# An S4 and SwiGLU layer on one core: other order and other first factors at the start of the kernel

## The reference, cut to what matters

```python
x  = u.reshape(2048, 512)                       # 2 x 1024 rows
xn = (x - mean(x)) / sqrt(var(x) + 1e-5)        # over 512 columns
# S4: a convolution along the 512 columns, kernel K from 64 complex states
B  = Vc @ Bp                                    # 64x64 complex by 64 real
K  = ifft(2/(1+Om) * (k00 - k01 * k10 / (1 + k11))).real   # Cauchy sums over Lambda, p, q, Ct, B
s  = causal_conv(xn, K) + D * xn
# FFN, hidden 1376, LoRA rank 16, scaling 2
lin(x, w, a, b) = x @ w.T + 2 * (x @ a.T) @ b.T
h  = silu(lin(xn, w1, A1, B1)) * lin(xn, w3, A3, B3)
out = x + s * silu(lin(h, w2, A2, B2))
```

## Time and profile before

| what | value |
|---|---|
| median of three runs | 411.93 us |
| the profiled execution, its own time | 412.15 us |
| its span, first to last instruction | 410.4 us |
| PE busy, records | 405.3 us (99%), 1860 |
| DVE busy | 164.9 us (40%) |
| ACT busy | 107.1 us (26%) |
| POOL busy | 66.8 us (16%) |
| DMA, whole span | 26.2 MB, mean 64 GB/s |
| granted TensorE clock by slice | 9 in all forty slices (9 is 90% or more) |

### The profile page before, as it was taken

How to read it: one execution, slowest core, us unless ns; L and a number is a source line. 1 busy time by engine, 2 the same in 40 slices (tenths; PEclk the granted TensorE clock), 3 DMA queues, 4 the chain that set the end, 5 groups by cost and what they waited for, 6 DMA issues and landing times.

```text
span 410.4 us, 5012 instructions
## 1 busy us (share of the span) xinstructions
PE 405.3 (99%) x1860; PEld 338.6 (83%) x1860; DVE 164.9 (40%) x259; ACT 107.1 (26%) x176; POOL 66.8 (16%) x130
## 2 busy tenths in 40 slices
PE   8999999999999999999999999999999999999996
PEld 8988888888888888888888888888888888888885
DVE  5777775654693321232244222132334212211125
ACT  7554333322441111122221111212222111111122
POOL 6227627330700114000000101400000000000000
PEclk9999999999999999999999999999999999999999
DMA  8663943220516101000006101000002000000002
GB/s 274 161 218 101 306 133 80 82 90 20 153 52 206 51 2 52 2 0 0 0 29 215 66 0 52 0 0 0 0 0 102 2 0 0 2 0 0 2 0 102
DMA packets 14338, 26.20 MB, mean 64 GB/s; under 512 B 2560, under 2 KB 4608, under 8 KB 14320
## 3 DMA queue, kind: packets, MB, share of 16 engines
q1 hardware_dynamic: 13872, 24.85, 18.9%
q0 software_dynamic: 160, 0.59, 0.4%
q10 hardware_dynamic: 288, 0.52, 0.3%
HBM read 20.33 MB, written 4.53 MB: 61 GB/s over the span
## 4 chain that ended last, share of the span: by engine, by line
PE 91%; DVE 4%; DMA 2%; issue 1%; ACT 1%; SPq 0%; POOL 0%; DVEq 0%; POOLq 0%
PE h L936 19%; PE h L935 19%; PE h L934 19%; PE f L935 10%; PE f L934 10%; PE f L936 10%; PE h L957 2%; DMA trig_sb<-trig_dram 2%; PE h L965 1%; PE spare L921 1%; DVE raw L732 1%; DVE w L747 1%; PE spare L936 1%; PE spare L935 1%; PE spare L934 1%
## 5 line engine op out<-in xcount | busy, mean ns | idle before, releaser
L934 PE MATMUL h<-xt,w 128*128 (+2 forms) x340 | 131.5, 387 | 0.0
L935 PE MATMUL h<-xt,w 128*128 (+2 forms) x340 | 131.1, 386 | 0.0
L936 PE MATMUL h<-xt,w 128*128 (+2 forms) x340 | 131.1, 386 | 0.0
L936 PEld LDWEIGHTS h<-xt,w 128*128 128x128 f32 x340 | 63.9, 188 | 12.8
L935 PEld LDWEIGHTS h<-xt,w 128*128 128x128 f32 x340 | 63.9, 188 | 12.7
L934 PEld LDWEIGHTS h<-xt,w 128*128 128x128 f32 x340 | 63.9, 188 | 12.6
L796 DVE TENSOR_TENSOR g<-g,h 128x512 f32<-128x512 f32 x40 | 27.5, 688 | 111.1 <-PE h L936 110.9
L801 DVE TENSOR_TENSOR ghl<-g,ghl 128x512 fp32r<-128x512 f32 x44 | 31.6, 719 | 92.5 <-ACT ghl L625 92.5
L934 PE MATMUL f<-ghl,w2f 128*128 128x512 f32 x176 | 68.6, 390 | 0.0
L625 ACT CAST ghl<-g 128x512 fp32r<-128x512 f32 x44 | 27.3, 621 | 157.9 <-PE f L936 144.7
L935 PE MATMUL f<-ghl,w2f 128*128 128x512 f32 x176 | 68.6, 389 | 0.0
(11 more groups left out here) (131 smaller groups left out, 306.2 us busy)
## 6 DMA issues: line engine op xcount, KB each, us to landing
raw<-w_dram SPq DMA_DIRECT2D x28, 256.0 KB, 3.4
xres<-xT_dram SPq DMA_DIRECT2D x4, 1024.0 KB, 7.2
outT_dram<-xres SPq DMA_DIRECT2D x15, 256.0 KB, 2.4
rows_next<-x_dram SPq DMA_DIRECT2D x4, 512.0 KB, 3.6
scale_rows<-scales_scratch SPq DMA_DIRECT2D x3, 512.0 KB, 4.1
rows<-x_dram SPq DMA_DIRECT2D x2, 512.0 KB, 6.8
raw<-w_dram SPq DMA_DIRECT2D x4, 224.0 KB, 2.4
lora_stack<-lora_spread_split SPq DMA_DIRECT2D x3, 204.0 KB, 3.7
```

The costliest lines, as they stand in the source:

```text
L934: pe.matmul(out, w[1], m[0], start=start, stop=False)
L935: pe.matmul(out, w[0], m[1], start=False, stop=False)
L936: return pe.matmul(out, w[0], m[0], start=False, stop=stop)
```

## The change

Seven edits, which all concern block 0:

1. Tile 0 of w2 joins `FOLD_FIRST`: it is folded with plain factors. `lr` grows from 1536 to 2176 columns, and its clearing with it; DVE clears 1216 columns for 832.
2. `folds`: (2,0) leaves the gate of j = 1, and (3,3) moves from the up of j = 2 to the down of j = 1.
3. SP: the raw tile (1,0) is loaded ahead of the first factors, not behind them; trig and the raw tile (2,1) are loaded ahead of the six stacking DMAs.
4. ACT and DVE: the order of their work up to the first hidden tile.
5. TensorE: the order of `start()`, with `fold(2,0)` in it.
6. Bp and Vc: two products over 64 partitions for one over 128.
7. `TOEPLITZ_AT` from (9, "up") to (8, "up"), and POOL's second `rows_rstd(1, 2)` behind the split of tz.

```diff
-FIRST_COLS = {1: 2 * D, 3: 2 * D + 2 * P}
-LORA_FIRST = 2 * D + 4 * P
+FIRST_COLS = {1: 2 * D, 3: 2 * D + 2 * P, 2: 2 * D + 5 * P}
+LORA_FIRST = 3 * D + 5 * P
-FACTORS_BY_DVE = 832
-PLAIN = {1: 1, 3: 1, 2: -1}
+FACTORS_BY_DVE = 1216
+PLAIN = {1: 1, 3: 1, 2: 0}
-FOLD_FIRST = [(1, 0), (3, 0), (1, 1), (3, 1)]
+FOLD_FIRST = [(1, 0), (3, 0), (1, 1), (3, 1), (2, 0)]
     if j == 1:
-        return {"gate": [(2, 0), (1, 2)], "up": [(3, 2), (1, 3)], "down": [(2, 1)]}[place]
-    if j == 2:
-        return {"gate": [(1, 4)], "up": [(3, 3), (3, 4)], "down": [(2, 2)]}[place]
+        return {"gate": [(1, 2)], "up": [(3, 2), (1, 3)], "down": [(2, 1), (3, 3)]}[place]
-TOEPLITZ_AT = (9, "up")
+TOEPLITZ_AT = (8, "up")
...
@@ sync
             load_tile(0)
+            load_raw(1, 0)
             sync.wait_ge(factors_dve, 1)
             sync.wait_ge(factors_pool, 1)
             sync.dma_start(lr[0:P:STACK_STEP, :], lora).then_inc(lora_in, 16)
             sync.dma_start(lane_c[:, :], lanes).then_inc(const_in, 16)
-            load_raw(1, 0)
...
             sync.dma_start(vc_sb[:, :], s4_vc).then_inc(bvec_in, 16)
+            sync.dma_start(trig_sb[:, :, :].rearrange("p a l -> p (a l)"), trig.to_broadcast([P, 2 * D])) \
+                .then_inc(s4_in, 16)
+            load_raw(2, 1)
...
-            early = [(1, 2), (3, 2), (1, 3), (2, 1), (3, 3)]
-            for kind, j in early[:2]:
-                load_raw(kind, j)
-            sync.dma_start(trig_sb[:, :, :].rearrange("p a l -> p (a l)"), trig.to_broadcast([P, 2 * D])) \
-                .then_inc(trig_in, 16)
-            for kind, j in early[2:]:
+            early = [(1, 2), (3, 2), (1, 3), (3, 3)]
+            for kind, j in early:
                 load_raw(kind, j)
@@ scalar
+            rows_hi(0)
             fold_hi(1, 0)
-            rows_hi(0)
+            rows_hi(1)
+            fold_hi(3, 0)
             act.wait_ge(spread_in, 32)
             nc.scalar.copy(spread_hl[:, 0, :], spread[:, :]).then_inc(spread_hi, 1)
             rows_norm(2)
-            rows_hi(1)
             rows_norm(3)
-            fold_hi(3, 0)
             rows_hi(2)
+            fold_hi(1, 1)
             rows_hi(3)
-            fold_hi(1, 1)
             fold_hi(3, 1)
+            fold_hi(2, 0)
             hidden(0, 0)
@@ vector
             fold_add(3, 0)
+            rows_lo(0)
             fold_lo(1, 0)
-            rows_lo(0)
+            rows_lo(1)
             dve.wait_ge(spread_hi, 1)
             nc.vector.tensor_tensor(spread_hl[:, 1, :], spread[:, :], spread_hl[:, 0, :].bitcast(F32), ALU.subtract) \
                 .then_inc(spread_lo, 1)
-            rows_lo(1)
             fold_lo(3, 0)
+            fold_add(1, 1)
+            fold_add(3, 1)
             rows_lo(2)
             rows_lo(3)
-            fold_add(1, 1)
-            fold_add(3, 1)
             fold_lo(1, 1)
             fold_lo(3, 1)
+            fold_add(2, 0)
+            fold_lo(2, 0)
             hidden_mul(0, 0)
@@ tensor, start()
                 fold(1, 0)
-                fold(3, 0)
                 pe.wait_ge(const_in, 16)
                 turn_rows(0)
+                fold(3, 0)
+                turn_rows(1)
                 fold(1, 1)
-                turn_rows(1)
-                fold(3, 1)
-                turn_rows(2)
 
                 pe.wait_ge(whi_done, 1)
                 pe.wait_ge(xhi_done, RT // 2)
...
-                turn_rows(3)
+                fold(3, 1)
                 wait_split(pe, 1, 0)
                 pe.wait_ge(xlo_done, RT // 2)
...
+                turn_rows(2)
+                turn_rows(3)
                 wait_split(pe, 3, 0)
                 hidden(0, 0, 0, 3, h3, lo)
+                fold(2, 0)
                 pe.wait_ge(xlo_done, RT)
                 hidden(0, 0, 0, 1, h1, hi).then_inc(h1_ready, 1)
...
-                pe.matmul(bankt[:, 0:2], vc_sb[:, :], bp_sb[:, :], start=True, stop=True).then_inc(b_ready, 1)
+                for ri in range(2):
+                    mm = pe.matmul(bankt[:, ri:ri + 1], vc_sb[:, ri * P:(ri + 1) * P], bp_sb[:, :], start=True, stop=True)
+                mm.then_inc(b_ready, 1)
@@ gpsimd
             rows_rstd(1, 0)
-            rows_rstd(1, 2)
             pool.wait_ge(tz_hi, 1)
             tt(tzs[:, 1, :], tz[:, :], tzs[:, 0, :].bitcast(F32), ALU.subtract).then_inc(tz_lo, 1)
-            pool.wait_ge(tz_lo, 1)
+            rows_rstd(1, 2)
```

More of the change, by code:

```diff
@@ L140 @@
 STACK_STEP = P // R
-FACTORS_BY_DVE = 832
-PLAIN = {1: 1, 3: 1, 2: -1}
-A_FIRST = {1: 0, 3: D}
-FOLD_FIRST = [(1, 0), (3, 0), (1, 1), (3, 1)]
+FACTORS_BY_DVE = 1216
+PLAIN = {1: 1, 3: 1, 2: 0}
+A_FIRST = {1: 0, 3: D, 2: 2 * D + 4 * P}
+FOLD_FIRST = [(1, 0), (3, 0), (1, 1), (3, 1), (2, 0)]
 def folds(place, j):
@@ L279, in build @@
         scales = put("scales", [P, 2, RT])
-        bp_sb = put("bp_sb", [P, 2])
+        bp_sb = put("bp_sb", [NS, 1])
         scal = put("scal", [P, 2])
@@ L308, in build @@
         even_odd = put("even_odd", [P, 2, D // 2])
-        vc_sb = put("vc_sb", [P, P])
+        vc_sb = put("vc_sb", [NS, 2 * P])
         krow = put("krow", [P, P + D])
@@ L347, in build @@
         spread_in, stack_in, stack_cleared = sem("spread_in"), sem("stack_in"), sem("stack_cleared")
-        s4_in, trig_in, bvec_in, dft_in = sem("s4_in"), sem("trig_in"), sem("bvec_in"), sem("dft_in")
+        s4_in, bvec_in, dft_in = sem("s4_in"), sem("bvec_in"), sem("dft_in")
         res0_in, res_in = sem("res0_in"), sem("res_in")
@@ L525, in _ @@
             sync.dma_start(spread[:, LANES_ST:LANES_ST + LANES_MV], lora_mv).then_inc(spread_in, 16)
-            for kind, j in FOLD_FIRST[2:] + [(2, 0)]:
+            for kind, j in FOLD_FIRST[2:]:
                 load_raw(kind, j)
@@ L539, in _ @@
                                    spread_hl[:, hl, lane_cols].bitcast(F32)).then_inc(stack_in, 16)
-            early = [(1, 2), (3, 2), (1, 3), (2, 1), (3, 3)]
-            for kind, j in early[:2]:
-                load_raw(kind, j)
-            sync.dma_start(trig_sb[:, :, :].rearrange("p a l -> p (a l)"), trig.to_broadcast([P, 2 * D])) \
-                .then_inc(trig_in, 16)
-            for kind, j in early[2:]:
+            early = [(1, 2), (3, 2), (1, 3), (3, 3)]
+            for kind, j in early:
                 load_raw(kind, j)
             sync.dma_start(dft_sb[:, :, :], dft).then_inc(dft_in, 16)
-            later = [f_ for f_ in FOLDS[len(FOLD_FIRST):] if f_ not in early + [(2, 0)]]
+            later = [f_ for f_ in FOLDS[len(FOLD_FIRST):] if f_ not in early + [(2, 1)]]
             for kind, j in later[:6]:
@@ L659, in body @@
                         if first and (j, place) == (1, "gate"):
-                            act.wait_ge(trig_in, 16)
+                            act.wait_ge(s4_in, 16 * 3)
                             act.wait_ge(small_ready, 1)
@@ L912, in fold @@
                 fac = lr if plain else lst
-                if (kind, j) == FOLDS[len(FOLD_FIRST)]:
+                if (kind, j) == (1, PLAIN[1] + 1):
                     pe.wait_ge(stack_in, 2 * len(STACK) * 16)
@@ L1188, in fold_lo @@
                 pool.wait_ge(wlo_pool, POOL_LO.index((kind, j)) + 1)
-            pool.wait_ge(s4_in, 16 * 2)
+            pool.wait_ge(s4_in, 16 * 3)
             then(ts(small[:, MINUS_LOG_STEP:MINUS_LOG_STEP + 1], scal[:, 1:2], -1.0, ALU.mult))
@@ L1321 @@
                          twice(p[:, 0]), twice(p[:, 1])], axis=1)
-    vct = vc.transpose(2, 1, 0).reshape(2 * NS, NS)
-    vct = _np.concatenate([vct, vct], axis=1)
-    bp = _np.asarray(L0_attn_Bp)
-    no = _np.zeros_like(bp)
-    bp = _np.concatenate([_np.concatenate([bp, no]), _np.concatenate([no, bp])], axis=1)
+    vct = vc.transpose(1, 2, 0)
+    vct = _np.concatenate([vct[:, 0], vct[:, 0], vct[:, 1], vct[:, 1]], axis=1)
     a1, b1, a3, b3, a2, b2 = (_np.asarray(a) for a in (L0_ffn_lora_A1, L0_ffn_lora_B1, L0_ffn_lora_A3,
@@ L1335 @@
         "w1": c(turned_tiles(L0_ffn_w1)), "w3": c(turned_tiles(_np.asarray(L0_ffn_w3)[up])), "w2": c(_np.asarray(L0_ffn_w2).T),
-        "lora": _np.concatenate([a1, a3, b1.T[:, :2 * P], b3.T[:, :2 * P]], axis=1),
+        "lora": _np.concatenate([a1, a3, b1.T[:, :2 * P], b3.T[:, :2 * P], a2[:, :P], b2.T], axis=1),
         "lora_st": lora_st.reshape(P, LANES_ST),
         "lora_mv": lora_mv.reshape(P, LANES_MV),
-        "s4_lanes": c(lanes_d), "s4_vc": c(vct), "s4_bp": c(bp),
+        "s4_lanes": c(lanes_d), "s4_vc": c(vct), "s4_bp": c(_np.asarray(L0_attn_Bp)),
         "s4_scalars": c(_np.stack([_np.asarray(L0_attn_D), _np.asarray(L0_attn_log_step)], axis=1)),
```

## The result

The kernel after the change takes 414.94 us (median of four runs, 414.69 to 415.17); before, beside it, 411.96 (four runs). The ratio is 1.007 [1.0055, 1.0085]: slower by 3.0 us, where the forecast was slower by 0.7 and the range ended at 413.7. The profiled execution took 415.08 us for a span of 413.3; before 412.15 for 410.4, so 2.93 us are to be found in the two traces.

What follows compares the result with a forecast made beforehand. The prediction took TensorE's (PE's) matmul stream to bound the kernel. Opening +1.32, stacked fold -0.23 and third hole -0.42 summed to +0.67 us on 411.93, giving 412.6 us; range 411.5 to 413.7.

Steps and rivals of the forecast that it cites:

- The opening, +1.32: Up to tile 1 of the hidden units: start at 20.06 us for 18.74, +1.32, bounds of the term 19.7 and 20.4.
- product with Bp: In the opening: two matmuls for one, four records for two, +0.14 us, 0.28 in all.
- price of 0.15 on DVE's first addition: In the opening: later first factors delay DVE's first add from 7.52 to 7.67 us; price between 0.05 and 0.5.
- All of it is on the path, since PE is the path: PE's added work, w2 tile 0's plain fold (0.87 us) included, counts in full: sum +0.78 us.
- The hole goes: minus 0.42: At 34.29 us: folds (3,3), (3,4) waited for the add of (1,4) on one bank; moving (3,3) earlier saves 0.42.
- cover of 0.7 for fold (3,3): The earlier (3,3) needs the add of (1,3), done at 28.9 us, at 29.6: cover 0.7.
- ACT's three denominators start sooner, and POOL ends them sooner: With trig earlier and one fold fewer at the gate; PE never waited for that chain, so nothing is gained.
- The stacked fold's -0.23: Later in block 0: w2 tile 0's one-record stacked fold leaves PE, minus 0.23 us.
- Toeplitz split one place earlier ... price nothing: The split and POOL's second scale set behind it are off PE's path before and after; price nothing.
- B, faster: Rival: new order closes the opening's holes, 411.1 us, if low rows 1 are done by 11.7; chance 0.10.
- C, the clock: Rival: PE's faster record spacing comes only after the second fold, +1.1, 413.7 us; chance 0.10.
- D, stack late: Rival: stack lands behind trig and w2 tile 1, so the first stacked fold waits; 0.7 given, 413.3 us; chance 0.13.

Runs made afterwards that it cites:

- a_bp: Kernel after the change with the product of Vc and Bp in one matmul over 128 partitions again; 414.16 us.
- b_order: Kernel before with only the new order of PE, ACT and DVE up to the first hidden tile, without the plain fold; 412.72 us, ratio 1.0019.
- a_f20: Kernel after with w2's tile 0 folded on the stack at the gate of j = 1 and first factors 1536 columns wide again; 413.88 us.
- a_fill: Kernel after with DVE's low rows 2 and 3 ahead of its add of w3's tile 1, ACT's high rows 3 ahead of w1 tile 1's high part; 414.74 us.
- b_fill: b_order with DVE's low rows 2 and 3 ahead of w3 tile 1's add, ACT's high rows 3 ahead of w1 tile 1's high part; 412.30 us, ratio 1.001.
- a_raw: Kernel after with w1's raw tile 0 loaded behind the first factors again; 414.95 us.
- a_f33: Kernel after with fold (3,3) back at the up of j = 2; 413.65 us.
- a_wait: Kernel after with POOL's first 512-column product (den_im) also waiting until DVE has written the low part of w1 tile 2; 414.05 us.
- a_toep: Kernel after with the Toeplitz split back at (9, up) and POOL's second scale set back ahead of it; 414.41 us.
- b_toep: Kernel before with only the Toeplitz split moved to (8, up) and POOL's second scale set behind tz's low part; 412.62 us, ratio 1.0012.
- a_trig: Kernel after with trig loaded behind the stack and two raw tiles again; median 413.80 us, five runs in two groups.
- best2: Kernel before with DVE's add of (1,4) ahead of the low part of (2,1), and low rows 1 ahead of the spread factors' split; 412.13 us, ratio 1.0002.

## Why the prediction was wrong

The forecast was +0.7 with its sum +1.32 - 0.23 - 0.42; measured was +1.75 - 0.22 + 0.61 + 0.56, and some 0.2 spread over the rest, whose cause is open. Two terms of the sum failed in their mechanism, the fold move (-0.42) and the Toeplitz split (nothing); the opening was right in its order of events and too small in two sizes.

**The opening, +1.32: mechanism right, size off by 0.43.** The order of events holds to a few hundredths up to 16.8: DVE's first add 7.66 (7.67), mixed matmuls 12.52 (12.52), low rows done 16.74 (16.68), PE on at 16.80 (16.82). Behind that two terms were too small. Twelve matmuls after a wait and up to the product with Bp took 1.62, not 1.44, and the product took 0.53, not 0.28. Its price came from the two records of before, with 0.07 each, while the four over 64 partitions are 0.13 apart on average; with the records next to it the change of the product costs 0.49 (a_bp, b_order: 3.20 us for 3.69), not 0.14. The factors landed at 6.33 (5.95); their price of 0.15 on DVE's first addition was right to 0.1.

**"All of it is on the path, since PE is the path": failed for the plain fold.** 0.87 us were counted, and the total was near only because the same sum contained the wait behind it: by the prediction's own 16.68 for the low rows PE would have stood still without the fold as long as it worked with it. That was luck in the number. a_f20 without the fold has the same opening behind the mixed matmuls, and a_fill with the wait taken away gains 0.2 where b_fill gains 0.65. What set the end of the opening was the new order of PE, ACT and DVE (0.93, b_order), then the later mixed matmuls (12.52 for 12.19 in b_order: 0.33) and Bp (0.49); the stretch in which the fold lies, from the mixed matmuls to the end of the wait, takes 4.28 us in both. Of the 0.33 some 0.25 is the wait of DVE's first addition for the late factors (see a_raw), the rest the start of DVE's chain, which differs by as much between profiles.

**"The hole goes: minus 0.42": failed, and the sign turned.** The old hole did go, but two new ones of 0.54 + 0.10 and 0.28 + 0.10 came. The cover of 0.7 for fold (3,3) was worked out with DVE at 0.68 per low part; the low part of (1,2) took 1.73 because POOL was at work. The step that made POOL start earlier stands in the prediction, "ACT's three denominators start sooner, and POOL ends them sooner ... so nothing is gained": it asked only whether PE waits for that chain, not what else the chain meets on its new date. The old hole, too, was put down to the shared bank alone, though what made DVE's addition late in it was POOL (see a_f33). a_wait, a_f33 and a_f20 each remove the loss, a_wait most of it, by another of its conditions.

**"Toeplitz split one place earlier ... price nothing": failed by 0.56.** It was left at nothing because the operations moved are off PE's path. They are, but POOL's held DVE's low part for 1.80 instead of 0.69, and that is on it. It is the same omission and the same mechanism, shown from both sides (a_toep, b_toep).

The trace of before had the sign of it. DVE's low part at 28.49, not among the rows shown, is 1.38 long for 0.68, beside POOL's product at 28.03:

```profile
28.49 1.38 DVE L747 TENSOR_TENSOR w<-raw,w 128x512 fp32r<-128x512 f32 x1 [0.51 <-ACT w L585]
```

```profile
28.03 1.29 POOL L1145 TENSOR_TENSOR den_im<-den_im,res 128x512 f32<-128x512 f32 x1 [14.00 <-ACT res L664]
```

28.03 + 1.29 + 0.55 = 29.87 = 28.49 + 1.38. A look for the longest members of a group, and not only its mean, would have found it.

**The rivals.** B, faster: the condition (low rows 1 by 11.7) wasn't met, they ended at 12.37. C, the clock: not in the median, but one profiled execution shows the wider spacing, at about 0.9 for 1.1, with a granted clock of 1.00 all the same. D, stack late: it landed at 21.97 (forecast 21.4), before the first stacked fold at 23.24, so nothing waited. Nor did trig delay it: in a_trig, with trig behind it, the stack landed at 21.90. PE did wait for the stack in b_fill and best2, where trig is behind it as well. The stacked fold's -0.23 came as forecast, -0.22. The true case, two engines that hold each other up, wasn't among them, and the range was too narrow by that.

## What to carry to other kernels

When an edit moves an operation in time on an engine that nobody waits for, list what runs beside it at the new time, not only who waits for it: here two moves of POOL's work, by 0.5 and by 8.1 us, cost PE about 1.5 us, against the same kernel without them. A gap in the bounding engine's stream is a place, not a loss to be added up: work put into it is free (the plain fold), and work done earlier in front of it comes back as waiting (the mixed matmuls). An experiment that takes one wait away must be read for the wait that takes its place (a_raw). And a cover of a few tenths should be checked against the longest instance of the operation that must fit into it.

## What the runs showed of the hardware

- A two-input SBUF operation of DVE (512 columns, 0.68 us) that starts within a running POOL operation of 512 columns ends 0.55 us after POOL's end: 1.73, 1.56 and 1.38 us here, and 1.80 for the pair of 320 columns, with a lead of POOL of 0.04 to 0.62 us. If DVE leads (by 0.41, a_f20), DVE keeps 0.68 and POOL takes 1.42 for 1.30. DVE operations with one input in PSUM are not touched (0.68 to 0.69 beside POOL).
- Four fp32 records over 64 partitions with one column each take 0.53 us on PE, the two over 128 partitions with two columns 0.14.
- PE's fp32 records of 128 columns are 0.21 us apart until 5 to 7 us from the start, in one profiled execution until 10.3, and then 0.11, with a granted clock of 1.00 in the records throughout. What decides it, the runs don't show. PE waited 0.80 for the factors in the kernel after and 0.85 in that execution of a_fill; but in the kernel after the spacing had narrowed ahead of that wait (the 22 filler records took 4.58 us), and in a_fill it hadn't (5.06).
